# A decoder block whose expert routing is done in two phases, with the last pairs of its first stage written out

## What is computed

```
x = layernorm(x + retrieve(x))      # v = x Wv^T; cumsum over tokens of v*exp(i t f), turned back, times Wo^T
x = layernorm(x + retention(x, ctx))  # (x ctx^T / 16) * decay, rows divided by max(|row sum|, 1), times ctx
x = layernorm(x + moe(x))           # 8 experts, the best 2 of each token, gates a softmax over those 2
```

## Time and profile before

| | us |
|---|---|
| median of 3 runs | 251.29 (250.74 to 251.42) |
| the profiled execution, its own time | 253.51 |
| its span, first to last instruction | 251.6 |
| first stage up to the last logits | 0 to 104.6 |
| routing, up to the first gather | 104.6 to 119.05 |
| expert loop, up to the last scatter's landing | 119.05 to 230.7 |
| results back, last norm, stores | 230.7 to 251.6 |

### The profile page before, as it was taken

How to read it: one execution, slowest core, us unless ns; L and a number is a source line. 1 busy time by engine, 2 the same in 40 slices (tenths; PEclk the granted TensorE clock), 3 DMA queues, 4 the chain that set the end, 5 groups by cost and what they waited for, 6 DMA issues and landing times.

```text
span 251.6 us, 4803 instructions
## 1 busy us (share of the span) xinstructions
PE 209.8 (83%) x1403; PEld 186.0 (74%) x1403; DVE 165.2 (66%) x496; ACT 107.0 (43%) x268; POOL 150.9 (60%) x137
## 2 busy tenths in 40 slices
PE   7857979999999999877899999999999999991000
PEld 7746879889899888876788888887788888870000
DVE  3946688988988788488256565565465655650384
ACT  3251324424523411355255445554454545540094
POOL 0364659668677531056736777767777777643580
PEclk9979999999999999996899999999999999998555
DMA  6954456776775101101222332323333233311995
GB/s 229 398 208 167 108 188 170 246 233 173 238 192 172 42 1 44 43 1 5 84 63 78 110 94 84 101 74 105 105 99 96 73 107 99 101 38 31 416 364 191
DMA packets 17238, 33.78 MB, mean 134 GB/s; under 512 B 4829, under 2 KB 7648, under 8 KB 17216
## 3 DMA queue, kind: packets, MB, share of 16 engines
q1 hardware_dynamic: 12752, 21.78, 26.4%
q0 software_dynamic: 3744, 9.35, 12.7%
q10 hardware_dynamic: 720, 2.36, 2.4%
HBM read 25.08 MB, written 9.32 MB: 137 GB/s over the span
## 4 chain that ended last, share of the span: by engine, by line
PE 43%; DVE 16%; POOL 14%; issue 10%; DMA 10%; ACT 4%; POOLq 1%; SPq 0%; DVEq 0%; ACTq 0%
POOL y_dram L1037 7%; PE p_c L558 6%; POOL keep L1018 6%; PE p_y L474 6%; DMA keep<-x_dram,gather_idx 5%; DMA space<-y_dram 4%; PE p_v L413 3%; PE p_c L431 3%; PE p_v L558 3%; PE p_s L458 3%; PE p_a L493 2%; PE p_r L502 2%; PE p_v L402 2%; PE p_c L402 2%; DVE x L668 2%
## 5 line engine op out<-in xcount | busy, mean ns | idle before, releaser
L1037 POOL DMA_INDIRECT y_dram<-keep,scatter_idx x39 | 39.5, 1013 | 19.4 <-issue 10.1
L1018 POOL DMA_INDIRECT keep<-x_dram,gather_idx x39 | 38.1, 978 | 15.3 <-issue 9.1
L558 PE MATMUL p_c<-w_hi,parts 128*128 x104 | 34.6, 414 | 0.0
L835 DVE TENSOR_TENSOR cs<-p_c,cs 128x256 f32<-128x256 f32 x26 | 11.0, 424 | 25.2 <-ACT cs L947 25.2
L1003 POOL TENSOR_TENSOR w_lo<-keep,w_hi 128x1536 fp32r<-128x1536 f32 (+1 forms) x8 | 27.5, 3439 | 0.0
L935 ACT ACTIVATE parts<-p_y 128x256 fp32r<-128x256 f32 x39 | 15.0, 385 | 27.0 <-PE p_y L584 27.0
L828 DVE TENSOR_TENSOR parts<-p_y,parts 128x256 fp32r<-128x256 f32 x39 | 16.5, 424 | 7.0 <-ACT parts L935 6.6
L994 POOL TENSOR_TENSOR cs<-space,vinv 128x256 f32<-128x256 f32 x16 | 9.5, 616 | 18.9 <-DVE vinv L737 15.3
L474 PE MATMUL p_y<-wo,space 128*128 128x256 f32 x64 | 17.3, 418 | 2.8 <-POOL space L986 2.8
L558 PEld LDWEIGHTS p_c<-w_hi,parts 128*128 128x128 f32 x104 | 17.7, 189 | 2.3
L947 ACT ACTIVATE cs<-p_c 128x256 f32<-128x256 f32 x26 | 10.0, 386 | 20.0 <-PE p_c L558 20.0
(11 more groups left out here) (173 smaller groups left out, 531.3 us busy)
## 6 DMA issues: line engine op xcount, KB each, us to landing
keep<-in_weights SPq DMA_DIRECT2D x8, 768.0 KB, 4.6
space<-in_xT SPq DMA_DIRECT2D x8, 256.0 KB, 3.3
keep<-in_x SPq DMA_DIRECT2D x8, 256.0 KB, 3.3
space<-in_ctxT SPq DMA_DIRECT2D x8, 256.0 KB, 3.4
space<-in_ctxt SPq DMA_DIRECT2D x8, 256.0 KB, 3.3
x_dram<-x SPq DMA_DIRECT2D x8, 256.0 KB, 3.7
space<-y_dram SPq DMA_DIRECT2D x4, 512.0 KB, 7.8
space<-y_dram ACTq DMA_DIRECT2D x4, 512.0 KB, 8.1
```

What stands on the lines that cost most here:

```text
L558: last = nc.tensor.matmul(dst, lhs[:, k, :], w[:].rearrange("p e n -> p (e n)")[:, bass.ds(start + col + k * width, width)], start=(n == 0 ...
L1018: nc.gpsimd.indirect_dma_start(xs[k % HELD], None, x2_dram, bass.IndirectOffsetOnAxis(ap=gather_idx[:, k:k + 1], axis=0)).then_inc(xs_ok[k ...
L1037: nc.gpsimd.indirect_dma_start(y_dram, bass.IndirectOffsetOnAxis(ap=scatter_idx[:, k - 2:k - 1], axis=0), xs[s][:, 0:D], None, bounds_chec ...
```

## The change

**Two phases of routing.** The first ten batches (EB) are selected, ranked and inverted by themselves. Of each expert only the full tiles are used, at most 13 (ET, the number that ten batches always fill) in all. The rest of their choices and the last six batches (LB) fill the 26 late tiles (LT). The total stays at 39. The early masks are 20 pieces: eight by ACT (now as |row - r| and a Relu, two steps each), seven by POOL, five by DVE. The late selection stands after the early index arithmetic and before the loop. The rest of the late routing is a function `late_routing(k)` that DVE calls at the end of loop iterations -1 to 11; ACT builds eight late masks in iterations 0 to 7, DVE four; TensorE runs the late inverse, 32 products of 26 columns, in iteration 8 (LATE_INVERSE), before the down product of that iteration. From tile 13 on, POOL, TensorE and ACT wait once more for the late indices, and POOL for the late gates as well.

**The last pairs written out.** `pipeline` now ends with step 6; what steps 7, 8 and 9 did is written out for each engine in an order of its own. Selection of the ten early batches is put between the steps of pairs 6 and 7. Some work changes engine: residuals of pair 7 are added by TensorE (a product with the unit matrix), half of some normalisations and of cs goes to ACT. `FILL` goes; 2, 2 and 7 fillers stand in the drain, and 11, 8 and 4 in the routing. x2_dram gets one row more at its front, for padding rows of a tile.

The core of the diff (first the constants, then SP, TensorE, DVE, ACT and POOL):

```diff
+EB, LB = 10, 6
+NE, NL = TOPK * EB, TOPK * LB
+ET = -(-(EB * T * TOPK - E * (P - 1)) // P)
+LT = TILES - ET
+LATE_INVERSE = 8
+
+ACT_EARLY, POOL_EARLY, DVE_EARLY = (0, 1, 2, 3, 10, 11, 12, 13), (4, 5, 6, 7, 14, 15, 16), (8, 9, 17, 18, 19)
+ACT_LATE, DVE_LATE = (20, 21, 22, 23, 24, 26, 27, 28), (25, 29, 30, 31)
 
...
+            for j in range(PAIRS - 3, PAIRS):
+                sp.wait_ge(x2_ok, j + 1)
+                if j == PAIRS - 1:
+                    sp.wait_ge(x2b_ok, 1)
+                sp.dma_start(x2_pairs[j:j + 1].rearrange("a t q d -> t (a q) d"), x2[j % 2][:]).then_inc(x2_out[j % 2], 16)
+                if j == PAIRS - 3:
+                    sp.wait_ge(x2_out[1], 48)
+                    sp.sem_inc(x2_free, 1)
+
+            def store_gates(first, end):
+                for q in range(2):
+                    sp.dma_start(gate_rows[:, first // 2:end // 2, q, :],
+                                 gate_pair[:].rearrange("p (j q) c -> p j q c", q=2)[:, first // 2:end // 2, q, :]).then_inc(
+                                     gates_saved, 16)
+
+            sp.wait_ge(gate_ok, 2)
+            store_gates(0, EB)
+            for s in range(2):
+                sp.wait_ge(x2_out[s], 64)
             sp.sem_inc(x2_saved, 1)
-            sp.wait_ge(gate_ok, 2)
-            for q in range(2):
-                sp.dma_start(gate_rows[:, :, q, :], gate_pair[:].rearrange("p (j q) c -> p j q c", q=2)[:, :, q, :]).then_inc(
-                    gates_saved, 16)
+            sp.wait_ge(gate_ok, 4)
...
+            nc.tensor.matmul(r1_7[0], ident, x_in[1][:, 0, :], start=False, stop=True)
+            nc.tensor.matmul(r1_7[1], ident, x_in[1][:, 1, :], start=True, stop=False)
+            pe.wait_ge(got_ok, 8)
+            last_y(1, False, True).then_inc(y_ok, 1)
+            pe.wait_ge(cT_ok[0], 64)
+            pe.wait_ge(x1T_ok, 7)
+            pe.wait_ge(att_ok, 6)
+            score(6).then_inc(sc_ok, 1)
+            keep_busy(2, ident, "c")
+            pe.wait_ge(att_ok, 7)
+            pe.wait_ge(logits_ok, 5)
+            row_sums(att).then_inc(sum_ok, 1)
...
+            score(7).then_inc(sc_ok, 1)
+            pe.wait_ge(cs_ok, 7)
+            for q in range(2):
+                last = nc.tensor.matmul(p_y[:, q, :], att[:, q, :], cs[:, q, :], start=True, stop=True)
+            last.then_inc(av_ok, 1)
...
+            pe.wait_ge(chosen_ok, 1)
+            before(place_e[:, 0:1, :], 0, 1, True)
+            above(place_e[:, 1:, :], 0, True)
+            before(place_e[:, 1:EB, :], 1, EB, False)
+            for b in range(1, EB):
+                last = above(place_e[:, b + 1:, :], b, False)
+            last.then_inc(place_ok, 1)
...
+            router(plog, x2T).then_inc(lg_ok, 1)
+            pe.wait_ge(x2_ok, 7)
+            transposes(p_t, x2[0]).then_inc(t2_ok, 1)
+            keep_busy(7, ident, "c")
+            pe.wait_ge(x2_ok, 8)
+            pe.wait_ge(x2b_ok, 1)
+            pe.wait_ge(x2T_ok, 7)
+            transposes(p_t, x2[1]).then_inc(t2_ok, 1)
+            pe.wait_ge(logits_ok, 6)
+            router(plog, x2T).then_inc(lg_ok, 1)
+            pe.wait_ge(x2T_ok, 8)
+            router(plog_7, x1T).then_inc(lg_ok, 1)
+
+            for b in range(EB):
+                above(place_l, b, b == 0)
+            keep_busy(11, ident, "t")
+            pe.wait_ge(tile_is_ok, 1)
+            for c in range(TOPK):
...
+                    last = nc.tensor.matmul(inv_e[c], row_hot[:, n, :], tile_is_e[:, n, :],
+                                            start=(n == names[0]), stop=(n == names[-1]))
+            last.then_inc(inv_ok, 1)
+            keep_busy(8, ident, "t")
             pe.wait_ge(chosen_ok, 2)
-            before(0, 1, True)
-            above(0, True)
...
-            for b in range(B - LATE, B):
-                last = above(b, False)
+            before(place_l[:, 0:LB, :], EB, B, False)
+            for b in range(EB, B):
+                last = above(place_l[:, b - EB + 1:, :], b, False)
             last.then_inc(place_ok, 1)
...
-            keep_busy(20, ident, 1)
...
-            keep_busy(12, ident, 1)
+            keep_busy(4, ident, "t")
             pe.wait_ge(index_ok, 1)
...
+                        pe.wait_ge(rank_ok, 2)
...
+                        pe.wait_ge(tile_is_ok, 3)
+                        for c in range(TOPK):
+                            names = [*range(c * EB, (c + 1) * EB), *range(NE + c * LB, NE + (c + 1) * LB)]
+                            for n in names:
...
+                                                 start=(n == names[0]), stop=(n == names[-1]))
+                    if k == LATE_INVERSE + 3:
+                        pe.wait_ge(gather_ok, 2)
                     split_product(p_down[s], hid_hi[s], hid_lo[s], W_DOWN, D, down_at).then_inc(down_ok, 1)
...
+            numbers(inv_e, early)
+            select(1, 0, 3)
+            select(1, 0, 4)
+            select(1, 0, 5)
+            select(1, 1, 0)
+            shift_by_top(EB, B)
+            for part_no in range(1, 6):
+                select(1, 1, part_no)
+            for part_no in range(3):
+                targets(inv_e, early, part_no)
+            dve.wait_ge(place_ok, 2)
+            note("placed", nc.vector.tensor_tensor(placed[:, NE:, :].rearrange("p (c b) e -> p c b e", c=TOPK), picks[1],
...
+            def late_routing(k):
+
+
+                if k == -1:
+                    note("full", nc.vector.tensor_tensor(full[:], caps[:, 1, :], caps[:, 0, :], ALU.subtract))
+                    after_op("rank")
+                    note("part", nc.vector.tensor_scalar(part[:, NE:], rank[:, NE:], -HALF, 1.0 / P, ALU.add, ALU.mult))
+                    after_op("full")
+                    note("upto", nc.vector.tensor_tensor(upto[0][:, E:], offset_e[:], full[:], ALU.subtract))
+                    after_op("part")
+                    note("tile_in", nc.vector.tensor_scalar(tile_in[:, NE:], part[:, NE:], ROUND, -ROUND, ALU.add, ALU.add))
+                    running(0)
+                    after_op("tile_in")
+                    nc.vector.scalar_tensor_tensor(row_no[:, NE:], tile_in[:, NE:], -float(P), rank[:, NE:],
+                                                   ALU.mult, ALU.add).then_inc(row_no_ok, 1)
+                if k == 0:
...
+                    gates(EB, B, 0)
...
+                if k == 3 or k == 4:
+                    rows = slice(0, TOPK * B // 2) if k == 3 else slice(TOPK * B // 2, TOPK * B)
+                    after_op("tile_no")
+                    nc.vector.tensor_tensor(tile_is_l[:, rows, :],
+                                            half[:, H_ROW:H_ROW + LT].unsqueeze(1).to_broadcast([P, TOPK * B // 2, LT]),
+                                            tile_no[:, rows].unsqueeze(2).to_broadcast([P, TOPK * B // 2, LT]),
+                                            ALU.is_equal).then_inc(tile_is_ok, 1)
...
+                if k == 5:
+                    make_row(DVE_LATE[0])
+                    make_row(DVE_LATE[1])
+                if k == 6:
+                    make_row(DVE_LATE[2])
+                    gates(EB, B, 3)
+                if k == 7:
+                    make_row(DVE_LATE[3])
+                    gates(EB, B, 4)
+                if k == LATE_INVERSE:
+                    numbers(inv_l, late)
+                    targets(inv_l, late, 0)
...
+                    nc.vector.tensor_scalar(expert_idx[:, ET:], expert[:, ET:], float(E - 1), float(W_END),
+                                            ALU.min, ALU.mult).then_inc(index_ok, 1)
+                    targets(inv_l, late, 1)
+                if k == LATE_INVERSE + 3:
+                    targets(inv_l, late, 2)
+
...
+                late_routing(k)
...
+                if place + 1 < len(ACT_EARLY):
+                    distance(ACT_EARLY[place + 1], place + 1)
+                make_row(ACT_EARLY[place], place)
...
+            act.wait_ge(half_in, 16)
+            act.wait_ge(row_no_ok, 1)
+            distance(ACT_EARLY[0], 0)
+            early_row(0)
             act.wait_ge(shift_ok, 1)
...
-            for n in ACT_ROWS:
-                nc.scalar.activation(off[:, n - ACT_ROWS[0], :], half[:, H_ROW:H_ROW + P], ACT.Abs,
-                                     bias=row_neg[:, n:n + 1]).then_inc(off_ok, 1)
-            act.wait_ge(off_ok, len(ACT_ROWS))
-            nc.scalar.activation(row_hot[:, ACT_ROWS[0]:, :], off, ACT.Relu, bias=const[:, C_ONE:C_ONE + 1],
-                                 scale=-1.0).then_inc(row_hot3_ok, 1)
...
+            act.wait_ge(lg_ok, 8)
+            nc.scalar.activation(logits[:, 14:16, :], plog_7, ACT.Copy).then_inc(logits_ok, 1)
+            for place in range(2, len(ACT_EARLY)):
+                early_row(place)
+            act.wait_ge(shift_ok, 2)
...
+                if 0 <= k < len(ACT_LATE):
+                    if k == 0:
+                        act.wait_ge(row_no_ok, 2)
+                    distance(ACT_LATE[k], len(ACT_EARLY) + k)
```

(34 more changed lines are left out.)

603 lines of the change are left out of this document (464 added, 139 removed).

## The result

The changed kernel takes **239.39 us** (median of 4 runs, 238.91 to 241.23) against 251.25 us before (250.74 to 251.42): a ratio of **0.9498, 95% interval 0.9449 to 0.9547**. Forecast were 243.4 us and a range of 239.5 to 247.3. The sign and the mechanism held; the gain is 11.9 us where 7.9 were forecast, and the time lies 0.1 us under the range.

A forecast was written before the change was run, and what follows sets the result against it. Routing delays the loop, where GpSimd sets the pace with TensorE close behind. From 251.29 us, -10.9 (earlier first gather) + 1.9 (clock) + 0.3 (fill) + 0.8 (inverse) = -7.9 gives 243.4, range 239.5 to 247.3.

The forecast's parts named there:

- Part one (drain): Last pairs written out: last x2 of pair 7 near 98.5 us, 3.0 earlier than 101.53.
- The 0.7 us for contention: Early selection steps slowed beside GpSimd's multiplication for cs: 0.7 us added before the first gather.
- Part three (clock): At the loop's start TensorE's clock falls and dense work runs at half speed: +1.9 us.
- Rival (b): The clock holds at the loop's start: 241.5 us, lowest 240.0; chance 0.20.
- the early bound: First gather 11.6 us earlier instead of 10.9, without contention: -0.7 us.
- a free inverse: The late inverse on TensorE in iteration 8 costs the loop nothing: -0.8 us.
- the hops: Short delays between steps, possibly counted twice in the drain: 0.5 us off the range's low end.
- Part two, the masks: Early routing: three engines build 20 masks, all level near 105; first gather 108.1 against 119.05, 10.9 us earlier.
- Part four (loop): Late routing inside the loop mostly hidden: +0.3 us for the fill, +0.8 for the late inverse.
- Rival (e): Late DVE and ACT steps add to the loop in series, slower than before: 257.3 us; chance 0.05.

The follow-up runs named there:

- the second profile: The changed kernel, unedited, run and profiled once more: ratio 0.9517 against the kernel before.
- masks 7 and 8: Changed kernel with one early row mask moved from ACT (7 instead of 8) to GpSimd (8 instead of 7): ratio 0.9547 against the kernel before.

## Why the prediction was wrong, by its steps

**Part one (drain) was mis-sized: -3.0 forecast, -4.7 measured.** The order of time of the changed kernel:

```profile
79.43 0.54 DVE L1002 TENSOR_SCALAR x<-p_y,mv,rs 128x256 f32<-128x256 f32 x1
...
82.25 1.03 PE L594 MATMUL p_v<-wo,space 128*128 128x256 f32 x4
...
85.11 0.56 ACT L1330 ACTIVATE x<-p_v,shift,rs 128x256 f32<-128x256 f32 x1 [0.43 <-DVE shift L980]
...
86.38 0.60 DVE L895 SCALAR_TENSOR_TENSOR masked<-pick,logits 128x80 f32<-128x80 f32 x1
...
87.22 1.13 PE L558 MATMUL p_s<-x1T,space 128*128 128x128 f32 x8
...
88.39 0.42 DVE L1033 TENSOR_TENSOR att<-p_s,const 128x256 f32<-128x256 f32 x1 [0.17 <-PE p_s L558]
...
91.93 0.17 DVE L902 TENSOR_TENSOR shifted<-top 128x20 f32<-128x20 f32 x1
```

Counted from the sums (79.39 in the forecast, 77.59 here), x1 of pair 6 ends at 2.4 (forecast 2.4), y at 5.7 (6.0), x1 of pair 7 at 8.1 (8.4), its scores at 10.8 (11.2). Up to here the shapes' durations carry. Then DVE's own queue takes 3.7 us (88.39 to 92.10) where I summed 4.6 to 4.9. A row begins before the one ahead of it on its engine has ended, so back-to-back steps cost less than the sum of their durations (the fifteen rows here add up to 4.2, with 0.3 of idle time between them besides), and I had added hops on top, and took 0.29 for selection steps of 0.23. After that 2.9 instead of 3.1.

**The 0.7 us for contention did not lie on the path.** It happened: L895 takes 0.60 beside GpSimd's multiplication for cs, as the earlier trace rows had it. But it ends while DVE would be waiting for the scores: DVE still idles 0.17 before L1033. The first gather came 26.7 us after the sums, 28.7 forecast (108.1 - 79.39): 1.7 of this miss of 2.0 is the drain, and these 0.7, less some 0.4 that row_no and the masks gave back, are the rest.

**Part three (clock) was the step that failed in kind: +1.9 forecast, no cost measured.** I let the fall begin in the rest before 111.2 and so under the loop's products. In the first profile it began near 103.3, after rests of only 0.2 to 0.5 us between drips of narrow products, and was over before the first tile; in the second, with the same rests up to there, it didn't come. What decides stays open: the long rests that I compared with don't tell these two apart. By the rows of the run without fillers the price was of about the right size for the case that I had in mind. Rival (b), the clock that holds, came nearest (241.5, and 240.0 with the early bound), for the reason that the second profile shows and not the first. The range missed because its low end, with a clock that holds, no contention and a free inverse, let the drain itself gain only 0.5 more than forecast (the hops), and it gained 1.7 more.

**Part two, the masks,** came out nearly right (7.95 for 7.7) by two errors: ACT's step costs 0.34 us (0.67 for a mask of two) rather than 0.30, and the exponential and two logit copies, for which I had 0.59, put its masks off by only some 0.24. GpSimd's 1.072 us a mask was a mean that mixed two kinds. Before, two of the seven:

```profile
109.69 1.05 POOL L1012 TENSOR_SCALAR space<-half,row_no,const 128x128 f16<-128x128 f16 x1 [12.91 <-DVE row_neg L785]
...
110.74 2.08 POOL L1012 TENSOR_SCALAR space<-half,row_no,const 128x128 f16<-128x128 f16 x1
```

The second ran beside DVE's wide comparison of two inputs from memory (L792, 1.46 us from 110.86); the other five took 0.82 to 0.91. After the change, where no step that long runs beside them, seven take 5.60, 0.80 each. Another rule of the same section of the Trainium skill says that a DVE instruction with two SBUF inputs contends with a GpSimd one that reads SBUF. The row of 2.08 agrees with it, and the selection steps of the earlier trace rows are of that kind too; but shorter steps of that kind cost a mask next to nothing (L1091, 0.48 us, beside masks of 0.81 and 0.85, where one with no DVE step beside it takes 0.78; the comparison itself, now L1106, 0.48 us beside one of 0.82 in masks 7 and 8), and no run varies such a step alone. So the cause of the 2.08 is argued, not shown.

**Part four (loop) was right in size:** 0.5 for the fill where I had 0.3, 0.6 in GpSimd's queue for the inverse where I had 0.8, gather 13 without a wait (0.30), and late steps that the loop hides: in series the first scatter comes 9.4 us later, 6.8 of them ahead of the first transposes. Rival (e) falls with that.

## What to carry to other kernels

A sum of row durations overstates a dense queue: take the distance from start to start of a similar run of steps, and add contention only where the engine would not have waited anyway. When a change takes away idle-filling work, ask which work would run during a low clock: it costs where the dense products are and next to nothing where fillers are. Take a price from single rows, not from a group's mean, if another engine's neighbour changes.
